# The last group's routing moved into the first tiles of each mixture of experts

## The reference

```python
x = x + deltanet(layernorm(x))          # 4 heads, chunks, a triangular solve and a state
x = x + moe(layernorm(x))               # mixture 0
x = x + linear_recurrence(layernorm(x)) # a scan over 1024 tokens
x = x + moe(layernorm(x))               # mixture 1, same weights

def moe(x):                             # 8 experts, two for each token
    probs = softmax(x @ router_w.T)
    topk_probs, topk_idx = top_k(probs, 2)        # then normalised to sum 1
    h = gelu_new(x @ w_fc[e] + b_fc[e])           # 128 -> 512
    out = h @ w_proj[e] + b_proj[e]               # 512 -> 128
    return sum over the token's two experts of weight * out
```

## Time and profile before

| | |
|---|---|
| time, median of 3 runs | 1500.07 us (1498.42 to 1503.52) |
| the profiled execution's own time | 1501.17 us |
| its span in the profile | 1499.1 us |
| busy | PE 67%, DVE 77%, ACT 46%, POOL 53% of the span |
| mean granted TensorE clock | 0.777 of full speed |
| instructions | 33118 |

### The profile page before, as it was taken

The page is one execution under the profiler, slowest core; times in us unless marked ns, Lnnn a source line. Parts: engine busy times, 40 slices in busy tenths (PEclk is TensorE's granted clock), DMA queues, the critical chain, the costliest instruction groups (busy, mean ns, idle before and its releaser), DMA issues.

```text
span 1499.1 us, 33118 instructions
## 1 busy us (share of the span) xinstructions
PE 1010.0 (67%) x11963; PEld 743.7 (50%) x11963; DVE 1150.6 (77%) x3327; ACT 686.7 (46%) x1510; POOL 789.5 (53%) x668
## 2 busy tenths in 40 slices
PE   4446858677684546269999983655454459999970
PEld 1224545454454435157888871333222348888850
DVE  1198998888999874376888864999999767887855
ACT  2334344352433212146777853544344146877740
POOL 3232246565465443545666662166777755666660
PEclk9768859586685655578999995767766579999985
DMA  4011001111111100157878743011111357888739
GB/s 127 22 42 45 24 29 50 39 60 36 42 55 33 48 24 16 31 213 254 273 267 280 267 151 116 28 58 62 64 36 36 106 182 259 272 271 279 257 128 336
DMA packets 78625, 184.33 MB, mean 123 GB/s; under 512 B 16735, under 2 KB 44826, under 8 KB 68224
## 3 DMA queue, kind: packets, MB, share of 16 engines
q1 hardware_dynamic: 51280, 142.04, 28.3%
q0 software_dynamic: 17280, 35.70, 6.9%
q10 hardware_dynamic: 9904, 4.49, 1.1%
HBM read 131.20 MB, written 52.79 MB: 123 GB/s over the span
## 4 chain that ended last, share of the span: by engine, by line
PE 45%; DVE 30%; POOL 7%; issue 7%; ACT 5%; DMA 3%; SPq 2%; POOLq 0%; DVEq 0%; ACTq 0%
PE ps L1489 5%; PE ps L1697 4%; PE ps L1698 4%; PE ps L1699 4%; PE ps L1709 4%; PE ps L1711 4%; PE ps L1710 4%; DVE seq L1133 3%; POOL rn L607 2%; PE ps L1685 2%; DVE prod L781 2%; POOL xs L624 2%; PE ps L1630 2%; DVE t_p L789 2%; PE ps L1719 2%
## 5 line engine op out<-in xcount | busy, mean ns | idle before, releaser
L624 POOL DMA_INDIRECT xs<-ysc,slot_u x256 | 277.3, 1083 | 226.7 <-DVE slot_u L904 153.9
L662 POOL DMA_INDIRECT res<-orow,idt x284 | 296.0, 1042 | 175.8 <-DVE orow L1069 103.8
L1061 DVE TENSOR_TENSOR hidl<-hidf,hidh 128x512 fp32r<-128x512 f32 (+1 forms) x320 | 200.2, 634 | 37.9 <-ACT hidh L1369 31.6
L1367 ACT ACTIVATE hidf<-ps,wb 128x512 f32<-128x512 f32 (+1 forms) x320 | 198.8, 655 | 3.9 <-PE ps L1699 2.1
L1697 PE MATMUL ps<-yTh,wb 128*128 128x512 f32 (+1 forms) x320 | 128.1, 400 | 0.0
L1709 PE MATMUL ps<-hidh,wb 128*128 128x512 f32 (+1 forms) x320 | 124.7, 390 | 0.0
L1698 PE MATMUL ps<-yTl,wb 128*128 128x512 f32 (+1 forms) x320 | 121.2, 379 | 0.0
L1699 PE MATMUL ps<-yTh,wb 128*128 128x512 f32 (+1 forms) x320 | 121.1, 378 | 0.0
L1711 PE MATMUL ps<-hidh,wb 128*128 128x512 f32 (+1 forms) x320 | 118.2, 369 | 0.0
L1710 PE MATMUL ps<-hidl,wb 128*128 128x512 f32 (+1 forms) x320 | 118.0, 369 | 0.0
L607 POOL TENSOR_TENSOR rn<-ss,neg_half 128x64 f32<-128x64 f32 x8 | 86.3, 10792 | 37.8 <-DVE ss L730 37.8
(11 more groups left out here) (257 smaller groups left out, 2586.7 us busy)
## 6 DMA issues: line engine op xcount, KB each, us to landing
wb<-wblob SPq DMA_DIRECT2D x80, 1032.0 KB
xt<-xs SPq DMA_DIRECT2D x62, 288.0 KB, 5.8
wblob<-hl SPq DMA_DIRECT2D x16, 512.0 KB, 3.0
fin<-res SPq DMA_DIRECT2D x14, 512.0 KB, 10.5
hidf<-res SPq DMA_DIRECT2D x10, 512.0 KB, 4.1
res<-orow,idt POOLq DMA_INDIRECT x284
xs<-ysc,slot_u POOLq DMA_INDIRECT x256
rs<-res SPq DMA_DIRECT2D x8, 512.0 KB, 4.7
```

Of the source, the lines that this page charges most:

```text
L624: pool.indirect_dma_start(xs[:, :], bass.IndirectOffsetOnAxis(slot_u[:, g % 2, k, n:n + 1], 0), ysc[:, g % 2, n, :], None).then_inc(s(f"mo ...
L662: pool.indirect_dma_start(res[m][:, :], bass.IndirectOffsetOnAxis(idt[:, t % IR, j:j + 1], 0), orow[:, t % OR, j, :], None, bounds_check=2 ...
L1061: ve.tensor_tensor(hidl[:, t % 2, c, 0:n], hidf[:, t % 2, c, 0:n], hidh[:, t % 2, c, 0:n].bitcast(F32), ALU.subtract)\
L1367: ins = act.activation(hidf[:, t % 2, c, 0:n], ps[:, c, 0:n], ACT.Gelu_apprx_tanh, bias=b_col)
```

## The change

The last group of each mixture (group 7, and group 15 of mixture 1) keeps only its `route_variances` and `route_power` where they were. The rest of its route is called from the steps of the mixture's first tiles: `route_rows` in step 0, `route_turn` in step 1, `route_logits` and `choose` in step 2, `route_ranks`, `weigh`, `place` and the new `route_ends` in step 3; its sends follow the result scatters of tiles 2 to 5 on POOL, four a tile. The delta loop's last pass ends at slot 13, the recurrence's loop loses its pass `b = 9`.

So that tiles can be formed without that group, `early_table` uses the counts of six groups instead of seven and forms 16 tiles instead of 8; it runs one pass earlier. `route_table` is cut in five pieces, called at the end of DVE's steps 5 to 9. `fill_ends` becomes `fill_end(e)`, two calls ahead of each of SP's tiles 9 to 12. SP no longer waits for the last group's `x` before the first loads. The nine short tiles, which used to be spread over tiles 8 to 39, are spread over tiles 16 to 39. The last group's logits and ranks get PSUM bank 7 for all their parts. Arrays are placed in another order, so that `wb` and `xt` lie over arrays that are dead by then. No arithmetic is added or left out.

```diff
-    N_EARLY = 8
+    N_EARLY = 16
...
-            return (BK_P,) * 4 if g < B else (0, 0, 1, 1)
+            return (BK_A,) * 4 if g % B == B - 1 else (BK_P,) * 4 if g < B else (0, 0, 1, 1)
...
-        TABLE_AT = 2
+        TAIL_ROWS, TAIL_TURN, TAIL_LG, TAIL_RANK, TAIL_SEND, TAIL_TABLE, TAIL_FILL = 0, 1, 2, 3, 2, 5, 9
...
-                    sp.wait_ge(s("d_x"), GPB * B)
+                    sp.wait_ge(s("d_inv"), B)
                 else:
-                    sp.wait_ge(s("l_x"), GPB * (B + 1))
+                    sp.wait_ge(s("r_took"), B)
...
-                sent(0, (m + 1) * B // 2)
-                sent(1, (m + 1) * B // 2 - 1)
+                for p in range(2):
+                    sent(p, (m + 1) * B // 2 - 1)
...
-                    if t - t0 == fill_at:
-                        fill_ends()
+                    if 0 <= t - t0 - TAIL_FILL < E // 2:
+                        for k in range(2):
+                            fill_end(2 * (t - t0 - TAIL_FILL) + k)
...
-                for t in range(SLOTS):
+                for t in range(SLOTS if i < B else R_Y):
...
+                    k = t - m * NT - TAIL_SEND
+                    if 0 <= k < BPB // 2:
+                        for n in range(2):
+                            send((m + 1) * B - 1, 2 * k + n)
...
-                if t == R_VAR + 1 and g == B - 1:
+                if t == R_VAR + 1 and g == B - 2:
...
-                    if t - t0 == TABLE_AT:
-                        route_table(m)
...
+                    if t - t0 == TAIL_LG:
+                        choose((m + 1) * B - 1)
+                    if t - t0 == TAIL_RANK:
+                        weigh((m + 1) * B - 1)
+                        place((m + 1) * B - 1)
+                        route_ends(m)
+                    if 0 <= t - t0 - TAIL_TABLE < 5:
+                        route_table(m, t - t0 - TAIL_TABLE)
...
-                    if b == B:
-                        early_table(1)
                     if b < B:
                         scans(b)
                         ratio(b)
-                    if 1 <= b <= B:
+                    if b == B - 1:
+                        early_table(1)
+                    if 1 <= b < B:
                         choose(B + b - 1)
...
+                    if t - t0 == TAIL_LG:
+                        route_turned(last, (1,))
                     if t + 1 < t1:
                         tokens_high(t + 1)
+                    if t - t0 == TAIL_RANK:
+                        route_tanh(last)
                     for c in range(HC):
                         if t < t1:
                             hidden(t, c)
+                    if t - t0 == TAIL_ROWS:
+                        route_rows(last)
+                    if t - t0 == TAIL_TURN:
+                        route_turned(last, (0,))
...
+                    if t - t0 == TAIL_TURN:
+                        route_turn(last, (0,))
+                    if t - t0 == TAIL_LG:
+                        route_logits(last)
+                    if t - t0 == TAIL_RANK:
+                        route_ranks(last)
                     if t >= t0 + 2:
                         back(t - 2)
                     if t0 < t <= t1:
                         down(t - 1)
+                    if t - t0 == TAIL_TURN:
+                        route_turn(last, (1,))
```

More of the change, by code:

```diff
@@ L283, in hybrid_kernel @@
         fin_ctx.close()
+        hidh = sb("hidh", [2, HC, GT], F32R)
+        hidl = sb("hidl", [2, HC, GT], F32R)
         wb = sb("wb", [XB, WB], F32R)
@@ L308, in hybrid_kernel @@
         carry = sb("carry", [B])
+        lin = sb("lin", [4, L])
+        l_yT, l_r0, l_r1, l_x = (lin[:, k, :] for k in range(4))
+        l_r = (l_r0, l_r1)
+        l_oT = sb("l_oT", [2, GT])
         wblob = nc.dram_tensor("wblob", [E, P, WB], F32, kind="Internal").ap()
@@ L472, in sm, with fill_end @@
                     return s(f"moe_{name}")
-                def fill_ends():
-                    sp.wait_ge(sm("ends"), m + 1)
-                    for e in range(E):
-                        end = sp.value_load(end_u[0:1, e:e + 1], min_val=0, max_val=SPARE - HT)
-                        sp.dma_start(xs[bass.ds(end, HT), :].rearrange("(p j) c -> p j c", j=HB), bc(filler[:, :], 1, HB))\
-                            .then_inc(sm("filled"), 16)
+                def fill_end(e):
+                    if e == 0:
+                        sp.wait_ge(sm("ends"), m + 1)
+                    end = sp.value_load(end_u[0:1, e:e + 1], min_val=0, max_val=SPARE - HT)
+                    sp.dma_start(xs[bass.ds(end, HT), :].rearrange("(p j) c -> p j c", j=HB), bc(filler[:, :], 1, HB))\
+                        .then_inc(sm("filled"), 16)
                 def entry(row, t):
@@ L516, in moe_sync @@
                         sp.wait_ge(sm("filled"), 16 * E * (m + 1))
-                        sent(1, (m + 1) * B // 2)
+                        for p in range(2):
+                            sent(p, (m + 1) * B // 2)
                         if m == 0:
@@ L674, in _ @@
             linrec_power(0)
-            for b in range(B + 2):
+            for b in range(B + 1):
                 for n in range(BPB):
@@ L1295, in route_rows, with route_turned @@
                 normalise(g % B * BPB, lambda j: ysc[:, g % 2, j, 0:D], r_rstd, r_shift, "moe_y")
-            def route_turned(g):
-                for half in range(GPB):
+            def route_turned(g, halves=range(GPB)):
+                for half in halves:
                     act.wait_ge(s("moe_yT"), g * GPB + half + 1)
@@ L1436, in linrec_scalar @@
                 gates(0)
-                for b in range(B + 2):
-                    if 1 <= b <= B:
+                for b in range(B + 1):
+                    if b >= 1:
                         output(b - 1, 0)
@@ L1610, in post, with route_turn @@
                     ins.then_inc(s("d_out"), 1)
-            def route_turn(g):
-                for half in range(GPB):
+            def route_turn(g, halves=range(GPB)):
+                for half in halves:
                     pe.wait_ge(s("moe_yf"), g * GPB + half)
```

137 lines of the change are left out of this document (70 added, 67 removed).

## The result

The changed kernel takes 1456.2 us (median of 4 runs, 1454.04 to 1457.64) against 1500.61 (1498.42 to 1503.52) for the kernel before beside it: a ratio of 0.9702, 95% interval [0.9681, 0.9723]. It is 44 us faster, and 3 us slower than predicted. The forecast, 1453 from 1500.07, is a ratio of 0.9686, which lies inside that interval. Run again beside the first experiments the kernel took 1459.65 (5 runs, ratio 0.9724 [0.9705, 0.9743]); that interval leaves 0.9686 out, so the gap to the forecast is real, if small.

A forecast was written before the change was run, and what follows sets the result against it. PE bounds the kernel inside a mixture, not at its start. Gains of 23.5 us in mixture 0 and 25.1 in mixture 1, less 1.5, make 47.1 from 1501.2: 1454.1, as median 1453; range 1447 to 1462.

The forecast's parts named there:

- the route off the path: At each mixture's start, the last group's route no longer delays tile 0: up(0) 17.6 and 19.2 us earlier.
- the fillers' hole: Three tiles into each mixture, PE's 8.92 and 9.42 us waits behind SP's fillers, plus low clock: 11.6 us saved each.
- the new wait: PE behind down(0), second transposes waiting for ACT's copy behind tile 1's gelus: 2.4 us, clock kept full.
- The start of mixture 0: DVE reaches tile 0's weights at 630.6, not 648.2; up(0) starts 17.6 us earlier, at about 632.7.
- up(0) to up(4) of mixture 0: First tiles: 11.6 us of waiting and low clock go, 5.7 us of PE work and waiting come in; gains 5.9.
- The start of mixture 1: Early table shifts DVE by 4.2 us; tile 0's rows land last, by a hair; up(0) 19.2 us earlier.
- up(0) to up(4) of mixture 1: First tiles of mixture 1: again 11.6 us go and 5.7 come in, gaining 5.9 us.
- rival (a): Clock falls at PE's wait for ACT's copy in both mixtures: 5 us lost, 1458; chance 0.2.
- DVE, fillers and loads: DVE's added work, SP's fillers and closer weight loads of the last 24 tiles: 1.5 us lost, bounds 0 and 8.
- costed at nothing: POOL's added sends, tiles 2 to 5: some 18 us of lag met by 18 us of cover, so no cost.
- rival (b): DVE bounds steps 2 to 9, or last 24 tiles' weights late: 3 to 5 us a mixture, 1459 to 1463; chance 0.16.
- Rival (c): POOL's backlog reaches `rows`, DVE and PE: 10 us a mixture at 2 us a send, 1473; chance 0.02.

The follow-up runs named there:

- the first experiments: First set of follow-ups, timed beside the kernel before: changed kernel again, ACT's copy sooner, table in one step, two sends per tile; 1459.65, 1452.63, 1465.33, 1473.73 us.
- table_soon: Changed kernel with eight finished-row buffers and ACT's copy sooner, plus mixture 1's early table ahead of the last group's scans: 1446.51 us, ratio 0.9621.
- one_table: Changed kernel with all five pieces of the late table at the end of DVE's step 5: 1465.33 us, ratio 0.9759.
- sends_thin: Changed kernel with two of the last group's sends behind each of eight tiles, not four behind each of four: 1473.73 us, ratio 0.9815.
- rows8: Changed kernel with eight buffers of finished rows instead of four, `l_oT` laid over `out_t`: 1454.05 us, ratio 0.9686.
- sends_3: Changed kernel with the last group's sends as 3, 3, 3, 3, 2, 2 behind tiles 2 to 7: 1456.03 us, ratio 0.9702.
- after_again: The changed kernel itself, unaltered, measured again as yardstick of the first set: 1459.65 us, ratio 0.9724 to the kernel before.
- short_late: Kernel before with only its nine short tiles moved to tiles 16 to 39: 1498.48 us, ratio 0.9978.

## Why the prediction was right, point by point

The two big terms, the route off the path and the fillers' hole, came out to within 0.5 us each, for the reasons given. The time missed the narrow forecast (1450 to 1456) by 0.2 us in the first measurement and by 3.7 in the second and lies inside the range of 1447 to 1462. The first measurement flatters the forecast: in its profiled execution the clock stayed at full behind the new wait in mixture 0, as predicted, and that was luck, since it fell in the other five executions that have this wait.

**The start of mixture 0** (17.6 us predicted): 17.55. DVE's new start at the end of the variances and PE's "free since its last wo matmuls" were right.

**up(0) to up(4) of mixture 0** (5.9): 6.87 in the first execution, 4.0 in the second (36.20 against 32.16). The new wait was to be 2.4 and was 2.86 and 2.83 (2.2 to 2.9 over all executions that have it); its place and its cause, ACT's copy behind the gelus of tile 1, were those predicted, and moving the copy removed it. What is left without the wait is 27.70, and the prediction's other terms give 36.2 - 11.6 + 3.3 = 27.9: the two old prices and PE's new work were sized rightly. The wait itself was priced by its length, 2.4; with the clock at full it cost 1.6 of the stretch (29.33 against 27.70), and 4.5 with the clock low (32.16).

**The start of mixture 1** (19.2): 18.70. DVE forms the early table in 4.7 us (1147.53 to 1152.19) where 4.2 were reckoned. SP starts the weights 1.2 us behind it and the rows at 1155.77, and PE's turn ends its wait 7.1 us later, at 1162.85. "Last, by a hair" was right both ways: the variances end at 1162.33, half a microsecond ahead of the rows, and in table_soon, where the table is out of the way, only about 1 us came back, and DVE set the start.

**up(0) to up(4) of mixture 1** (5.9): 4.55 and 4.9. The wait was 2.41, as predicted. What the step had wrong is the sentence "so I keep the clock full": it fell to 0.61 over four microseconds. This is rival (a), and it came true in part. Six executions have the copy at its late place (the two of the changed kernel, one_table, sends_thin, rows8, sends_3), which makes twelve such waits of 2.2 to 2.9 us; behind eleven the granted clock was between 0.50 and 0.66 over the next four microseconds, and behind one, mixture 0 of the first profile, it was 1.00. Its price can be read in mixture 0: up(0) to up(4) takes 29.33 with the clock at full behind the wait, and 30.7 to 32.2 in the five with it low, so 1.4 to 2.8 us, against the 2.2 to 2.7 that (a) had. (The largest belongs to the execution in which the clock was low longest: in after_again it is still 0.50 from 651 to 652, in one_table, whose wait ends at the same time, 0.97.) The Trainium skill, "TensorE: Matmul & The Clock Gate", in its section on oscillation, says that idle gaps between groups of matmuls let the gate halve the clock and the loop pays each time; these traces agree in eleven cases of twelve.

**DVE, fillers and loads** (1.5 us off in all, bounds 0 and 8): 3.8 us were lost, 2.0 and 1.8 behind tile 16. The size was off, and the larger part of the cause was not among the three: neither DVE (no PE wait on `yTl` in tiles 4 to 10), nor fillers, nor short tiles by themselves (short_late). It was the step "costed at nothing" for the sends, "it holds, barely". A smaller part is the weights of rival (b): in mixture 0 it is 5.91 us from up(31) to up(32), behind DVE's wait of 3.27 for weights, against 4.90 in short_late, and 6.20 from up(19) to up(20), behind its wait for landings, against 5.08. POOL's timeline of the changed kernel, the rows of its first late scatter, the last send and the first scatter at which it is again waiting for DVE:

```profile
668.81 1.13 POOL L666 DMA_INDIRECT res<-orow,idt  x1 [3.26 <-DVE orow L1084]
...
711.62 0.96 POOL L628 DMA_INDIRECT xs<-ysc,slot_u  x1 [0.30 <-issue]
...
772.25 1.12 POOL L666 DMA_INDIRECT res<-orow,idt  x1 [0.30 <-DVE orow L1084]
```

POOL is busy without a break for 103 us, 60 of them behind the last send. The lag was sized somewhat low: POOL starts tile 6's scatters, at 712.88, 20.7 us behind their `orow` (DVE, 691.46 and 0.68 long), and 21.4 in mixture 1, where 0.8 is usual, so it fell back by 20 and not 18. It was taken as harmless because 18 us of it met 18 us of cover; cover without a margin lets late landings through, and POOL then has to win back the lag tile by tile. With eight buffers 3.6 of the 3.8 us came back in one execution and about 2 in the mean of five. Rival (c), the same mechanism at its worst, would have ended slower than before from 2.9 us a send; a send took 1.09 and 0.3.

**Around it.** The sum was 47.1 and the span fell 44.5. By terms (a minus is less gain than forecast): mixture 0 up to up(4) +0.9, mixture 1 -1.9, the late parts -2.3, the rest of the program +0.7 (delta -1.3 us, end -0.4, between the mixtures +1.0). This last group is not explained; the stretch between the mixtures, 275.75 before and 276.75 after, runs from 275.2 to 277.9 over the executions of kernels that don't differ from one of the two there, so it tells little.

Of the signs named in the prediction, the first ups, the missing 9 us waits, the wait for `yTf` of about 2.4 and the fifth up 30 us behind the first (29.3, 31.3) came as said, "at full clock thereafter" did not. PE shows no wait behind the fillers (SP issues them in pairs, 1.9 to 2.1 us each time). Of the signs that were to say which term is wrong, three came: the low clock; DVE's 3.27 us for weights past tile 16; and a first wait for `xt` in mixture 1 of 4.89 us. The last was ill chosen, for by the prediction's own working the rows land last while PE has long been free, and up(0) of mixture 1 still came 18.70 us nearer to the recurrence's end.

## What to carry to other kernels

Work that stands alone at a joint between two stages can be laid into the steps of the next one even when the engine there is the bound: here 3.3 us of PE work came in and 18 us of standing went, twice. When such work is laid in, walk through every queue for two things, not one: who waits behind it, and who waits for its end further on; the sends had a buffer count on one side and a deadline at tile 16 on the other: two per tile missed the deadline, four per tile used up the buffers, and three gave nothing that can be measured. Where cover and lag come out equal, count it as a cost, and look for a buffer that is cheap to double. A copy or a small result for a shared PSUM bank goes ahead of the long work on its engine, since a wait of under 3 us of a full PE cost up to 4.5 us here (27.70 without it, up to 32.16 with it and the low clock behind it).

## What was not expected of the hardware

The clock fell behind waits of 2.2 to 2.9 us between dense matmuls in eleven of twelve cases, and it came back some 3 to 6 us behind the end of the wait (in the window behind the wait in mixture 1 of the changed kernel it averages 0.61, and the steps after it run at 1.00). In one of twelve it stayed at full, behind a wait of 2.86, the longest of the twelve. So the length of the wait doesn't set these apart, and what does isn't shown by these traces. In the kernel before, the gap in the earlier trace rows was 3.12 us long and led to 0.59.

An indirect scatter of 128 rows costs POOL 0.96 us most often, now and then up to 1.5, and 0.30 to the next. That is so in the delta layer of the kernel before, where the DMA queues carry 44 GB/s (470 to 520), and in mixture 0 of the changed kernel at 271 GB/s (665 to 690): the mean of the 16 sends there was 1.07, against 1.09 over all 256.
